# A two-layer graph network on one core: the second layer's gathers without a bound

## What is computed

```python
h = relu(layernorm(x))
c = concat([h[src], h[dst], rel[typ]]) @ W1 + b1            # a message of each edge
b = leaky_relu(c @ w2)                                      # a score of each edge
alpha = softmax of b over the edges that end in one node
x = x + leaky_relu(segment_sum(c * alpha, dst))             # first layer

h = relu(layernorm(x))
agg = segment_sum(h[src], dst)                              # second layer: a plain sum
x = x + where(a node has edges, agg, h)
```

## Time and profile before

| | us |
|---|---|
| median of 3 runs (1597.97 to 1598.8) | 1598.76 |
| the profiled execution | 1597.28 |
| its span, first to last instruction | 1593.7 |
| PE busy in the span | 1336.8 (84%) |
| DVE busy | 1339.9 (84%) |
| ACT busy | 1329.0 (83%) |
| POOL busy | 1122.1 (70%) |

### The profile page before, as it was taken

The page is one execution under the profiler, slowest core; times in us unless marked ns, Lnnn a source line. Parts: engine busy times, 40 slices in busy tenths (PEclk is TensorE's granted clock), DMA queues, the critical chain, the costliest instruction groups (busy, mean ns, idle before and its releaser), DMA issues.

```text
span 1593.7 us, 34231 instructions
## 1 busy us (share of the span) xinstructions
PE 1336.8 (84%) x11994; PEld 1295.7 (81%) x11995; DVE 1339.9 (84%) x3785; ACT 1329.0 (83%) x3500; POOL 1122.1 (70%) x970
## 2 busy tenths in 40 slices
PE   1489999999999999999999998276777777767676
PEld 0479999999999999999999997276767767767676
DVE  6669999999999999999999988566676677676776
ACT  0589999899988999999899995288888889888887
POOL 5678888878666777778777600577777777777772
PEclk9999999999999999999999999688998898888998
DMA  3565666667655666666666646458888888888865
GB/s 96 169 170 153 193 189 170 175 180 187 189 164 168 184 189 192 178 180 172 185 188 193 171 129 167 136 157 227 232 235 230 229 231 240 224 235 229 229 192 143
DMA packets 465883, 298.78 MB, mean 187 GB/s; under 512 B 32307, under 2 KB 434697, under 8 KB 465710
## 3 DMA queue, kind: packets, MB, share of 16 engines
q1 hardware_dynamic: 433950, 243.29, 54.9%
q0 software_dynamic: 31760, 53.30, 12.6%
HBM read 202.27 MB, written 104.34 MB: 192 GB/s over the span
## 4 chain that ended last, share of the span: by engine, by line
PE 34%; DVE 24%; POOL 18%; issue 8%; ACT 8%; DMA 4%; SPq 1%; POOLq 0%; DVEq 0%; ACTq 0%
POOL xe L1165 15%; DVE st L1265 5%; PE c_p L1671 4%; DVE sel L1382 4%; PE c_p L1672 4%; POOL xn L1165 3%; DVE lr L1491 3%; PE c_p L1674 3%; PE t_p L1659 3%; DVE ot L1369 2%; DVE xn L1501 2%; PE t_p L1658 2%; ACT cs L1601 2%; PE t_p L1657 2%; DMA xe<-x_d,idx 2%
## 5 line engine op out<-in xcount | busy, mean ns | idle before, releaser
L1156 POOL DMA_INDIRECT xe<-in_x,idx_t x516 | 660.5, 1280 | 209.8 <-issue 138.5
L1165 POOL DMA_INDIRECT xe<-x_d,idx x320 | 333.1, 1041 | 129.9 <-issue 94.5
L1580 ACT ACTIVATE an<-xn,nbias,rstd 128x128 f32<-128x128 f32 x783 | 326.7, 482 | 3.0 <-DVE nbias L1296 3.0
L1265 DVE BATCH_NORM_STATS2 st<-xe 128x6 f32<-128x256 f32 x434 | 171.1, 413 | 120.2 <-DMA xe<-x_d,idx 119.9
L1583 ACT ACTIVATE ae<-xe,nbias,rstd 128x128 f32<-128x128 f32 x522 | 226.3, 482 | 0.0
L1671 PE MATMUL c_p<-w1a,th 128*128 128x129 f32 x1044 | 215.8, 288 | 0.0
L1672 PE MATMUL c_p<-w1b,th 128*128 128x129 f32 x1044 | 202.6, 276 | 0.0
L1265 DVE BATCH_NORM_STATS2 st<-xn 128x6 f32<-128x256 f32 x440 | 169.7, 413 | 34.8 <-DMA xn<-x_d,idx 28.3
L1382 DVE TENSOR_SCALAR sel<-row,plc_t,alpha 128x256 f32<-128x256 bf16 x522 | 191.8, 407 | 3.4
L1718 PE MATMUL sb_p<-cs,selT 128*128 128x128 f32 x768 | 122.8, 335 | 68.7 <-ACT cs L1601 68.7
L1718 PEld LDWEIGHTS sb_p<-cs,selT 128*128 128x128 f32 x768 | 118.2, 247 | 73.3 <-ACT cs L1601 73.3
(11 more groups left out here) (213 smaller groups left out, 3582.0 us busy)
## 6 DMA issues: line engine op xcount, KB each, us to landing
xn<-in_x SPq DMA_DIRECT2D x130, 384.0 KB, 6.3
x_d<-xn SPq DMA_DIRECT2D x130, 384.0 KB, 7.8
xn<-x_d SPq DMA_DIRECT2D x194, 256.0 KB, 4.5
out<-xn SPq DMA_DIRECT2D x194, 256.0 KB, 3.5
plr<-place_d SPq DMA_DIRECT2D x65, 256.0 KB, 3.7
tyr<-types_d SPq DMA_DIRECT2D x65, 256.0 KB, 5.6
xe<-in_x,idx_t POOLq DMA_INDIRECT x522, 3.6
xe<-x_d,idx POOLq DMA_INDIRECT x320
```

Source lines behind the costliest of these rows:

```text
L1156: nc.gpsimd.indirect_dma_start(out=xe_of(u)[:, e, :], out_offset=None, in_=x, in_offset=bass.IndirectOffsetOnAxis(ap=idx_t[:, j:j + 1], ax ...
L1165: nc.gpsimd.indirect_dma_start(out=xe2_of(u)[:, e, :], out_offset=None, in_=x1_d, in_offset=bass.IndirectOffsetOnAxis(ap=idx2[:, j:j + 1], ...
L1265: return v.bn_stats(st[:, j % 2, c:c + 2, :].rearrange("p c t -> p (c t)"), rows_.rearrange("p r d -> p d r"))
L1580: a(an[:, u % 2, i, :], xs_of(u)[:, i, :], ACT.Relu, bias=nbias1[:, c:c + 1], scale=rstd1[:, c:c + 1])
```

## The change

The second layer's gathers lose the bound, and what made it useful goes with it: `width2`, `skip2` and the addition of 2^20. The source rows are copied as they are, so the edges behind a tile's span keep theirs and are fetched like the others. Their places are as before, so their one-hots are zero and they add nothing to any sum. The copy stands in the first step of a table's round, behind the subtraction that gives `pl2`; before, the source rows came two steps later.

```diff
@@ second layer's small tables
-        small2 = sb("small2", [P, 99], f32)
+        small2 = sb("small2", [P, 94], f32)
-        minus2, width2, at2 = small2[0:rows2, 84:89], small2[0:rows2, 89:94], small2[0:rows2, 94:99].bitcast(i32)
+        minus2, at2 = small2[0:rows2, 84:89], small2[0:rows2, 89:94].bitcast(i32)
-        pl2, skip2, idf2 = (spare2[0:rows2, k * P:(k + 1) * P] for k in range(3))
+        pl2, idf2 = (spare2[0:rows2, k * P:(k + 1) * P] for k in range(2))
@@ gather2
                         nc.gpsimd.indirect_dma_start(out=xe2_of(u)[:, e, :], out_offset=None, in_=x1_d,
-                                                     in_offset=bass.IndirectOffsetOnAxis(ap=idx2[:, j:j + 1], axis=0),
-                                                     bounds_check=last_row, oob_is_err=False
+                                                     in_offset=bass.IndirectOffsetOnAxis(ap=idx2[:, j:j + 1], axis=0)
                                                      ).then_inc(gathered.sems[u % XE2], 16)
@@ second_borders
-                            v.memset(width2[rows_, k:k + 1], float(SPANS[t][1] * P))
@@ second_tables
-                        b.mark(v.tensor_scalar(pl2, win2[:, :, 0], minus2[:, k:k + 1], None, ALU.add))
-                    if at == 1:
-                        b.settle()
-                        b.mark(v.tensor_scalar(skip2, pl2, width2[:, k:k + 1], None, ALU.is_ge))
-                    if at == 2:
-                        b.settle()
-                        v.scalar_tensor_tensor(idf2, skip2, SKIP, win2[:, :, 1], ALU.mult, ALU.add).then_inc(k_rows2, 1)
+                        v.tensor_scalar(pl2, win2[:, :, 0], minus2[:, k:k + 1], None, ALU.add)
+                        v.tensor_copy(idf2, win2[:, :, 1]).then_inc(k_rows2, 1)
```

## The result

| | before | after |
|---|---|---|
| median, us | 1598.78 (4 runs, 1597.97 to 1601.27) | 1580.68 (4 runs, 1580.09 to 1582.48) |
| ratio | | 0.9887, 95% interval 0.9876 to 0.9899 |
| span of the profiled execution, us | 1593.7 | 1576.1 |

The changed kernel is 18.1 us faster, 1.13%.

What follows compares the result with a forecast made beforehand. POOL's gathers were taken to bound the second layer. From the profiled 1597.3 us, 5.0 for gathers without the bound and 1.0 for DVE's work gave 1591.3, or 1592.8 on the median's scale; range 1582 to 1604, the forecast's own 1582 to 1595.6.

Steps and rivals of the forecast that it cites:

- What bounds the second layer: Second layer: POOL's 416 gathers and 415 issue gaps of 0.305 us make its 558 us; 1 ns a gather is 0.42 us.
- The price of the bound: Second layer's gathers on POOL: without the bound each takes 12 ns less than 1000, 5.0 us faster in all.
- the line from 87 over 121: Unbounded gathers of 87 and 121 partitions, 6.2 ns a partition, carried on to 128: 1010 ns, 4.2 us slower.
- The sign named for the first term: Second layer's gathers (L1165) at 980 to 990 ns in floor and median, gap 0.30 us, would confirm the 5.0 us gain.
- The bounds of the sum: Second layer's gathers without the bound: from 72 us faster, where ACT becomes the bound, to 22 us slower, at 1054 ns each.
- What speaks against a price: Bounded gathers skipping a quarter of their rows and those skipping 6% share a floor, so skipping shows no cost on POOL.
- The added bytes: Second layer's gathers fetch 1.3% more bytes, costed at nothing under POOL's beat; 7 us if DMA were the bound.
- DVE: First layer: memsets, comparisons and cheaper copies save 2.7 us of DVE time, counted as 1.0 us faster, between 0 and 2.7.
- A check that costs nothing: Rival: second layer's gathers stay within some 6 ns of 1000, 1597.8 us; no change, with still-skipped rows included, 0.36.
- A dearer gather without a bound: Rival: second layer's gathers take 1010 ns, 1602.0 us, or 1620 at 1054 ns each; chance 0.17.
- That the rows are still skipped: Rival: second layer's rows behind the span stay skipped, bytes at 23.5 MB, 1597.8 us; counted within no change, 0.36.
- The line over rows an engine: Second layer's gathers, drawn over 29, 11 and 8 rows an engine: 1019 ns at 128 partitions, 7.9 us slower, 1605.7 us.

## Why the prediction was half right

**What bounds the second layer: right.** 415 gaps of 0.305 us and 416 gathers made the stage before, and they make it now; the sum of the gathers fell by 18.3 us and the stage by 18.2, the span by 17.6, the median by 18.1. One ns is worth 0.42 us: the multiplier held.

**The price of the bound: the step that failed.** 12 ns were taken, 56 were measured in the median (53 with the bound put back on the same tables) and 44 in the mean. The direction was argued rightly, that an uneven number of partitions carries a cost which the line from 87 over 121 hands on to 128. Its size was not: "10 ns too much on that line" should have been 1010 - 944 = 66. Of these, 37 come from using the window's gather as the point at 121 (through the second layer's own 1022 and 1262 ns the line meets 128 at 973), and 29 are what uneven numbers add on top of that line. Staying near the row of the same shape was the choice that made the term small: that row had the check in it, so it could say nothing of the price of the check, and the 12 ns came from no row at all. The sign named for the first term, 980 to 990 ns in floor and median, did not show: they are 940 and 944. The bounds of the sum, 72 us faster to 22 slower, did hold the result, but the range was cut at 38 ns faster, for no reason that a row gave.

**What speaks against a price didn't.** "Gathers that skip a quarter of their rows and gathers that skip 6% have the same floor" is true, and the runs explain it: the price hangs on the check being carried, not on its verdict. Two cases that both carry the check can't show what it costs.

**The added bytes: right.** They came (25.06 MB) and cost nothing; the run with the bound back has them too and is no slower than before.

**DVE: too much.** 1.0 us was counted for memsets beside a PE that was not quite full. The first gather was to start about 1 us earlier and started at 1010.87 against 1010.75 us, and the run with the bound back, which keeps DVE's gain, measures 0.9998. DVE is busy 29.49 of 30 us from 440 to 470 with 99 instructions where it was as busy with 119, so other work of DVE filled the time.

**The rivals.** A check that costs nothing fell with the run that puts it back. A dearer gather without a bound fell at 128 rows (944 ns); 121 rows without a bound did cost 1022, but no run has 121 with a bound, and the number of rows is reason enough for it. That the rows are still skipped fell with the bytes. The line over rows an engine, 1019 ns and 7.9 us slower, which the prediction drew by the Trainium skill (DMA: Bandwidth & Descriptors, section "Why a DMA increments its semaphore by 16 and not by 1"), failed at 944 in the same way as mine: it took two gathers of uneven number, one of them the window's, for the base. By the other rule that it took from the Trainium skill (the same page, section "Anatomy of one DMA — SWDGE (gpsimd) path"), that making descriptors is small and completion is most of the fixed time, the edit would have been worth nothing. The trace disagrees: POOL is held 0.94 us by each gather, and 56 ns less of it in the median are this kernel's 18 us.

**What nobody forecast** is the 5.0 us lost again: the gathers beside one-hots grew dearer against their own median, 20.6 us over it instead of 15.6. The delay exists before and after. It doesn't strike more gathers: by the count above, 110 are long before beside the first and 105 after, but by 127 ns on average before and by 169 after. With the bound put back it is 108, by 137 ns, so the larger delay goes with the gathers that have no bound; why stays open. The first gather's part grew by 0.8 us, but not for want of the bound: with the bound back it is as long (3.94 us).

## What to carry to other kernels

Where one engine issues gather after gather and waits for nobody, every option that each instruction carries has a price times their number: take the bound off by making the row numbers valid, and expect nothing from it where the trace shows the issuing engine waiting. A price can be read only between rows that differ in the thing itself; when every row of the right shape has it, the honest range is as wide as the far rows. And look at what the vector engine does beside the gathers, since an operation that isn't on the path can still hold them.

## What the runs showed of the hardware

- The bound of an indirect gather of 128 rows of 512 bytes holds POOL for 53 to 56 ns of 997 to 1000, whether or not it finds anything to skip; the shortest gather of the first layer shows the same 53 ns.
- What a gather costs POOL doesn't go by the number of its partitions alone: 908, 933 and 944 ns for 64, 112 and 128, but 1022 for 121 and 1262 for 87.
- One-hot operations of DVE from SBUF to SBUF lengthen 80% of the gathers that have one beside their first 0.4 us, by 169 ns on average, and one gather by 3 us; with the source in PSUM none by more than 33 ns, with a second scalar 55% of them by 137 ns. Over 416 gathers that was 20.7 us of 413.3.
